# The last tile of a recommendation tower: an order of its own, four banks for its product rounds, its pair chunks one by one, and one store of all results as rows

## The chip, the core and the metric

One core of a Trainium2 chip. The core has a matrix engine (PE, called TensorE), a vector engine (DVE), an activation engine (ACT), a general engine (POOL, called GpSimd) and a queue engine that only issues transfers (SP, SyncE). They run at the same time and wait for each other on semaphores. The metric is the device time of one execution of the kernel in microseconds (us), smaller is better; a time is given as the median of several runs. Besides, one execution was recorded by the hardware profiler, and all rows below are from it.

## What is computed

For each of 2048 samples, 27 rows of 128 numbers are fetched from 27 tables by index. The rows and the products of every two of them (351 pairs), together with 16 context numbers, go through three dense layers:

```
e = stack([tbl_f[ids[:, f]] for f in range(27)], axis=1)      # 2048 x 27 x 128
inter = einsum('bfd,bgd->bfg', e, e)[:, TRIU_I, TRIU_J]        # 351 pair products
h = concatenate([e.reshape(2048, -1), inter, dense_ctx], 1)    # 3823 columns
h = maximum(h @ W_top1 + b_top1, 0)                            # 512
h = maximum(h @ W_top2 + b_top2, 0)                            # 256
y = h @ W_top3                                                 # 2048 x 1
```

## The kernel before

**Tiles and groups.** The samples are 16 tiles of 128 (numbered 0 to 15; tile 15 is `LAST`). The 27 features of a tile are 9 groups of three (`FEATS`, `GROUPS`). For each feature POOL issues one indirect gather (L240) of 128 rows of 512 bytes into a ring of six group buffers, so there are 432 gathers in 144 groups; POOL may run up to six groups ahead of PE's transposes.

**A group.** PE transposes its three features against the identity (`transpose_group`, L485) into a PSUM bank. ACT copies the bank twice: rounded to the high part (`copy_high`, L261) and whole into `emb` (`copy_whole`, L268). DVE then subtracts the high part, which gives the low part (`group_low`, L364). PE multiplies the group with its slice of the first layer's weights in three passes, high by high, high by low and low by high (`layer1_group`, L513 to L515, nine matmuls of 512 columns), and adds them up in the bank `p_hid1` of the tile.

**The pairs.** From `emb`, four rounds of small matmuls (`pair_products`, L573) make all products of a tile's samples in the two halves of `p_prod`, in turn; ACT copies one part of a round (`copy_first`, L287), DVE two parts (`copy_second`, L372). Once four rounds are copied, DVE transposes them in 32x32 blocks (`products_to_rows`, L378 and L379) and places the diagonals and the context columns as `pairs` (L382, L383). PE transposes the three chunks of `pairs` (L498, in the last tile L504), ACT and DVE split them into high and low, and PE multiplies them with the rest of the first layer's weights (`layer1_pairs`).

**The other layers.** DVE copies the finished `p_hid1` to `hid1` (`copy_hid1`, L400; in the last tile in halves, L411), PE transposes it (`transpose_hid1`, L544; last tile L551) into `p_hid1_t`, ACT adds the bias and cuts at zero (`relu1`, L304) and rounds (L308), DVE makes the low part (`hid1_to_low`, L404), PE does layer 2 (`layer2`, twelve matmuls of 256 columns, again L513 to L515), DVE layer 3 (`layer3`, L426 and L428). The result of a tile is one column of `y`, and SP stores it (`store_y`, L211): 128 partitions of 4 bytes each, 16 stores in all.

**The order.** All engines go through the same hand-written list of steps, `SEQUENCE`, for every tile: groups 0 to 6, the pairs of the tile before, groups 7 and 8. PE transposes two steps ahead of what it multiplies, in two banks in turn (`p_group`). Work of the tile before is hung on certain steps: rounds 1 to 3 of its products on groups 0 to 2, layer 2 of the tile before that on group 3, round 0 of the tile's own products and `transpose_hid1` of the tile before on group 8. The last tile has nobody behind it, so `last_tile` puts what is left after it. Each engine executes its own instructions strictly in the order written.

Of the kernel before, what the change touches and what calls it, by code (L numbers as in the profile page):

```python
# [11 lines left out]
P = 128  # L12
# [18 lines left out]
def dlrm_tower(nc, ids, tables, ctx_rows, w_dense, w_pairs, b1_t, w2, b2, w3, eye, out):  # L31
# [17 lines left out]
    FEATS = 3  # L49
# [13 lines left out]
    STEPS = len(SEQUENCE)  # L63
# [3 lines left out]
    out_t = out.rearrange("(t p) o -> t p o", p=P)  # L67

    with ExitStack() as ctx:
# [40 lines left out]
        y = sb("y", [P, TILES, 1])  # L110
# [6 lines left out]
        last_hid1_t = [p_hid1_t, p_group[1]]  # L117
# [34 lines left out]
        y_ready = sem("y_ready")  # L152

# [10 lines left out]
        LAST = TILES - 1  # L164
# [5 lines left out]
        def bank_of(g):  # L170
            return p_group[SEQUENCE.index(g) % 2][:, 0:FEATS, :]

        pairs_bank = p_group[SEQUENCE.index("pairs") % 2][:, 0:3, :]
        last_pairs_bank = [p_group[0][:, 0, :], p_prod[:, 0, 0:P], p_prod[:, 1, 0:P]]

        def steps(first_tile=0):
            return [(t, n) for t in range(first_tile, TILES) for n in SEQUENCE if t or n != "pairs"]
# [4 lines left out]
        diagonals = bass.AP(products, ROWS_Q, [[WIDE * ROWS_Q, P], [ROWS_Q + 1, NF], [ROWS_Q, DELTAS]])  # L182

        def round_products(r):

            return p_prod[:, r % 2, 0:BLOCKS * 2 * NF].rearrange("p (k u c) -> p u c k", u=2, c=NF)
# [7 lines left out]
        def _(sp):  # L194
# [30 lines left out]
            for t in range(TILES):  # L225
                store_y(t)
            sp.wait_ge(y_stored, TILES * 16)
# [18 lines left out]
        def _(act):  # L246
# [11 lines left out]
            def copy_high(t, g):  # L258
                s = t * GROUPS + g
                wait(act, group_used, s - SPLIT + 1)  # L260
                nc.scalar.activation(emb_high[:, s % SPLIT, :, :], bank_of(g),  # L261
                                     ACT.Copy).then_inc(group_high_done, 1)

            def copy_whole(t, g):
                if g == 0:
# [3 lines left out]
                                     bank_of(g), ACT.Copy).then_inc(group_copied, 1)  # L269
# [13 lines left out]
            def copy_first(t, r):  # L283
# [3 lines left out]
                nc.scalar.activation(round_columns(r), round_products(r)[:, 0], ACT.Copy).then_inc(first_copied, 1)  # L287

            def pairs_high(t):
                act.wait_ge(pairs_transposed, t + 1)  # L290
                wait(act, hid1_done, t)
                nc.scalar.activation(inter_high[:], pairs_bank, ACT.Copy).then_inc(inter_high_done, 1)
# [24 lines left out]
            order = steps()  # L317
            group_copies(0, 0)
            group_copies(0, 1)
            for k, (t, n) in enumerate(order):  # L320
                if k + 2 < len(order):
# [359 lines left out]
```

## Time and profile before

| | us |
|---|---|
| median of 3 runs | 590.93 |
| the runs | 589.64 to 592.48 |
| the profiled execution, whole | 588.81 |
| its span, first to last instruction | 586.7 |
| PE busy | 516.8 (88%) |
| POOL busy | 413.3 (70%) |
| ACT busy | 244.0 (42%) |
| DVE busy | 230.3 (39%) |
| granted TensorE clock, mean | 0.968 |

A share of busy time is a mean over stages that differ, and POOL's excludes the fixed stretch of about 0.3 us between two gathers. The time outside the span, 588.81 less 586.7, is 2.1 us.

### The profile page before, as it was taken

Reading aid. Unit: us, or ns where it says so; the run is one execution under the profiler, and the core shown is the slowest. Engines: PE = TensorE matmul, PEld = TensorE weight load, DVE = VectorE, ACT = ScalarE, POOL = GpSimd, SP = SyncE. Lnnn points to the kernel's source line nnn. Section 1 sums busy time; section 2 is a strip of 40 time slices with the busy share of each in tenths; the row PEclk is TensorE's granted clock in tenths of the full one; section 3 lists DMA queues with packets and bytes.
Section 4 is the critical chain, followed back from the end, with each engine's and each line's share of the span. In section 5 each row is a group of like instructions: output and inputs, shape, how many; then the busy total and the mean of one; then the engine's idle time right before and its main releaser. Section 6 shows DMA issues by size and latency. Waiting matters only on the chain.

```text
span 586.7 us, 10584 instructions
## 1 busy us (share of the span) xinstructions
PE 516.8 (88%) x4224; PEld 416.4 (71%) x4224; DVE 230.3 (39%) x476; ACT 244.0 (42%) x482; POOL 413.3 (70%) x436
## 2 busy tenths in 40 slices
PE   0668999799997989989899997999999997999973
PEld 0546787688786878778687785888787876878862
DVE  3662624324251343415134341534434241533442
ACT  3773544353433434343343432434443532444220
POOL 6777777777777777777777777777777777777200
PEclk9998999899998999989899997999999998999987
DMA  8873222423223242421525233241423233232000
GB/s 205 255 240 91 74 55 53 52 55 53 55 53 54 56 51 54 50 60 51 55 55 47 58 50 55 55 55 51 55 55 48 57 49 56 55 51 55 22 2 1
DMA packets 25748, 38.17 MB, mean 65 GB/s; under 512 B 14058, under 2 KB 14954, under 8 KB 25700
## 3 DMA queue, kind: packets, MB, share of 16 engines
q0 software_dynamic: 13824, 28.34, 26.6%
q1 hardware_dynamic: 11876, 9.16, 5.7%
q8 instruction: 34, 0.56, 0.4%
q14 instruction: 14, 0.11, 0.1%
HBM read 37.46 MB, written 0.01 MB: 64 GB/s over the span
## 4 chain that ended last, share of the span: by engine, by line
POOL 46%; PE 27%; issue 15%; DMA 9%; DVE 1%; ACT 0%; DVEq 0%; ACTq 0%; POOLq 0%
POOL gathered L240 46%; DMA gathered<-tbl_dram,idx 9%; PE p_hid L513 6%; PE p_hid L515 6%; PE p_hid L514 6%; PE p_prod L573 5%; PE p_group L485 3%; PE p_hid_t L544 1%; DMA idx<-ids_dram 0%; ACT hid L304 0%; ACT emb L268 0%; PE p_group L498 0%; DVE products L379 0%; DVE pairs L382 0%; PE p_hid_t L551 0%
## 5 line engine op out<-in xcount | busy, mean ns | idle before, releaser
L240 POOL DMA_INDIRECT gathered<-tbl_dram,idx x432 | 413.1, 956 | 133.7 <-issue 124.6
L364 DVE TENSOR_TENSOR emb_low<-p_group,emb_high 128x384 fp32r<-128x384 f32 x144 | 80.4, 558 | 292.4 <-ACT emb L268 291.6
L261 ACT ACTIVATE emb_high<-p_group 128x384 fp32r<-128x384 f32 x144 | 70.7, 491 | 282.6 <-PE p_group L485 282.6
L513 PE MATMUL p_hid<-w_high,emb_high 128*128 128x512 f32 x432 | 185.8, 430 | 0.0
L515 PE MATMUL p_hid<-w_high,emb_low 128*128 128x512 f32 x432 | 172.8, 400 | 0.0
L514 PE MATMUL p_hid<-w_low,emb_high 128*128 128x512 f32 x432 | 172.8, 400 | 0.0
L485 PE MATMUL p_group<-identity,gathered 128*128 128x128 f32 x432 | 78.0, 291 | 53.9 <-DMA gathered<-tbl_dram,idx 53.9
L268 ACT ACTIVATE emb<-p_group 128x384 f32<-128x384 f32 x144 | 125.1, 868 | 0.0
L485 PEld LDWEIGHTS p_group<-identity,gathered 128*128 128x128 f32 x432 | 51.8, 146 | 72.9 <-DMA gathered<-tbl_dram,idx 53.3
L515 PEld LDWEIGHTS p_hid<-w_high,emb_low 128*128 128x128 f32 x432 | 82.5, 191 | 20.0
L514 PEld LDWEIGHTS p_hid<-w_low,emb_high 128*128 128x128 f32 x432 | 83.6, 194 | 13.3
L513 PEld LDWEIGHTS p_hid<-w_high,emb_high 128*128 128x128 f32 x432 | 83.4, 193 | 13.4
L573 PEld LDWEIGHTS p_prod<-emb 128*64 128x64 f32 x2048 | 66.2, 140 | 24.8 <-issue 22.3
L573 PE MATMUL p_prod<-emb 128*64 128x54 f32 x2048 | 74.3, 227 | 2.3 <-ACT emb L268 2.3
L372 DVE COPY prod<-p_prod 32x216 f32<-32x216 f32 x128 | 48.8, 382 | 24.9 <-ACT prod L287 20.1
L287 ACT ACTIVATE prod<-p_prod 128x216 f32<-128x216 f32 x64 | 24.7, 387 | 6.6 <-PE p_prod L573 6.6
L355 DVE TENSOR_TENSOR w_low<-w_stage,w_high 128x512 fp32r<-128x512 f32 (+1 forms) x32 | 21.8, 693 | 10.0 <-ACT w_high L256 9.3
L256 ACT ACTIVATE w_high<-w_stage 128x512 fp32r<-128x512 f32 (+1 forms) x32 | 20.0, 635 | 11.2 <-DMA w_stage<-w_dense_dram 11.0
L513 PE MATMUL p_hid<-w_high,inter_high 126*128 126x512 f32 x48 | 21.8, 455 | 0.5 <-DVE inter_low L394 0.5
L514 PE MATMUL p_hid<-w_low,inter_high 126*128 126x512 f32 x48 | 20.6, 429 | 0.0
L515 PE MATMUL p_hid<-w_high,inter_low 126*128 126x512 f32 x48 | 20.3, 424 | 0.0
L513 PE MATMUL p_hid<-w_high,hid_high 128*128 128x256 f32 x64 | 18.3, 286 | 0.9 <-DVE hid_low L420 0.9
(48 smaller groups left out, 257.8 us busy)
## 6 DMA issues: line engine op xcount, KB each, us to landing
w_stage<-w_dense_dram SPq DMA_DIRECT2D x27, 256.0 KB, 3.4
gathered<-tbl_dram,idx POOLq DMA_INDIRECT x432
w_stage<-w_pairs_dram SPq DMA_DIRECT2D x3, 252.0 KB
w_stage<-w_dram SPq DMA_DIRECT2D x2, 256.0 KB, 5.0
out_dram<-y SPq DMA_DIRECT2D x16, 0.5 KB, 7.3
ctx_sb<-ctx_rows_dram SPq DMA_DIRECT2D x1, 216.0 KB, 6.7
idx<-ids_dram SPq DMA_DIRECT2D x1, 202.5 KB, 5.2
b_rows<-b_dram SPq DMA_DIRECT2D x1, 128.0 KB, 3.2
```

Source lines behind the costliest of these rows:

```text
L240: pool.indirect_dma_start(gathered[:, slot, k, :], None, tables[f], bass.IndirectOffsetOnAxis(ap=idx[:, t, f:f + 1], axis=0),).then_inc(gr ...
L261: nc.scalar.activation(emb_high[:, s % SPLIT, :, :], bank_of(g), ACT.Copy).then_inc(group_high_done, 1)
L268: nc.scalar.activation(emb[t % 2][:, :, f0:f0 + FEATS].rearrange("p b f -> p f b"), bank_of(g), ACT.Copy).then_inc(group_copied, 1)
L287: nc.scalar.activation(round_columns(r), round_products(r)[:, 0], ACT.Copy).then_inc(first_copied, 1)
L355: nc.vector.tensor_tensor(dst, src, high, ALU.subtract).then_inc(w_low_done, 1)
L364: nc.vector.tensor_tensor(emb_low[:, s % SPLIT, :, :], bank_of(g), emb_high_f32[:, s % SPLIT, :, :], ALU.subtract).then_inc(group_low_done, 1)
L372: nc.vector.tensor_copy(round_columns(r)[rows], round_products(r)[rows, 1]).then_inc(second_copied, 1)
L485: last = nc.tensor.transpose(bank_of(g)[:, k, :], gathered[:, slot, k, :], identity[:])
L513: nc.tensor.matmul(dst, high, w_high, start=start, stop=False)
L514: nc.tensor.matmul(dst, high, w_low, start=False, stop=False)
L515: return nc.tensor.matmul(dst, low, w_high, start=False, stop=stop)
L573: last = nc.tensor.matmul(p_prod[h * 2 * SLOT:(h + 1) * 2 * SLOT, r % 2, j * 2 * NF:(j + 1) * 2 * NF], x.rearrange("p b f -> p (b f)"), x[ ...
```

## The change

The steps of tiles 0 to 14 stay as they are. In the first 15 tiles only the stores are gone. What changes:

- **The last tile's order.** `LAST_SEQUENCE` puts the pairs of tile 14 after group 4 and not after group 6. Within the last tile PE transposes a group one step ahead and not two. `transpose_hid1` of tile 14 moves from behind group 7 to behind group 5, `layer2` of tile 14 from behind the last product round to ahead of the first one, and the multiplications of groups 7 and 8 move from ahead of and between the product rounds to behind all four.
- **Four banks.** The rounds 2 and 3 of the last tile's products go into the bank of tile 14's finished `p_hid1` and into `p_hid1_t`, so that no round waits for the copies of an earlier one.
- **Pair chunks one by one.** For the last tile ACT, not DVE, places the diagonals, in three pieces; the first needs only the first of DVE's two block transposes. PE transposes chunk 0 while it still has two features of group 8 to multiply.
- **One store.** `y` has 128 columns, of which 16 are used and the rest zeroed at the start. At the end PE transposes `y`, DVE copies 16 rows of 128 numbers to `y_rows`, and SP stores them with one transfer of 16 rows of 512 bytes.

```diff
-    STEPS = len(SEQUENCE)
+    LAST_SEQUENCE = [0, 1, 2, 3, 4, "pairs", 5, 6, 7, 8]
+    ORDER = [(t, n) for t in range(TILES) for n in (LAST_SEQUENCE if t == LAST else SEQUENCE) if t or n != "pairs"]
-    out_t = out.rearrange("(t p) o -> t p o", p=P)
+    out_t = out.rearrange("(t p) o -> t (p o)", p=P)
...
-        y = sb("y", [P, TILES, 1])
+        y = sb("y", [P, P])
+        y_rows = sb("y_rows", [TILES, P])
...
+        last_prod_bank = [p_prod[:, 0, :], p_prod[:, 1, :], p_hid1[(LAST - 1) % 2][:],
+                          p_hid1_t[:].rearrange("p c b -> p (c b)")]
...
-            def store_y(t):
-                sp.wait_ge(y_ready, t + 1)
-                sp.dma_start(out_t[t], y[:, t, :]).then_inc(y_stored, 16)
...
-            for t in range(TILES):
-                store_y(t)
-            sp.wait_ge(y_stored, TILES * 16)
+            sp.wait_ge(y_copied, 1)
+            sp.dma_start(out_t, y_rows[:]).then_inc(y_stored, 16)
+            sp.wait_ge(y_stored, 16)
...
+            def last_place_pairs(t):
+
+                for c in range(3):
+                    act.wait_ge(rows_done, 2 * t + min(c, 1) + 1)
+                    nc.scalar.activation(pairs[:, c * ROWS_I:(c + 1) * ROWS_I, 0:DELTAS], diagonals(c * ROWS_I, ROWS_I),
+                                         ACT.Copy).then_inc(last_placed, 1)
...
+                    if (ahead_t, ahead) == (LAST, GROUPS - 2):
+                        relu1(LAST - 1)
...
-            products_to_rows(LAST)
+            last_products_to_rows(LAST)
+            layer3(LAST - 1)
             last_pairs_low(LAST)
-            layer3(LAST - 1)
...
+            dve.wait_ge(y_transposed, 1)
+            nc.vector.tensor_copy(y_rows[:], y_bank[0:TILES, :]).then_inc(y_copied, 1)
...
+            def last_tile(t):
...
+                layer1_group(t, 3)
+                layer2(t - 2)
+                transpose_pairs(t - 1)
+                transpose_group(t, 5)
+                layer1_group(t, 4)
+                layer1_pairs(t - 1)
+                transpose_group(t, 6)
+                layer1_group(t, 5)
                 transpose_hid1(t - 1)
+                transpose_group(t, 7)
+                layer1_group(t, 6)
+                transpose_group(t, 8)
                 layer2(t - 1)
+                for r in range(ROUNDS):
+                    pair_products(t, r)
+                layer1_group(t, 7)
+                layer1_group(t, 8, [0])
+                last_transpose_pairs(t, [0])
+                layer1_group(t, 8, [1, 2])
+                last_transpose_pairs(t, [1, 2])
+                layer1_pairs(t, by_chunk=True)
                 last_transpose_hid1(t)
                 layer2(t, by_chunk=True)
+                pe.wait_ge(y_ready, TILES)
+                nc.tensor.transpose(y_bank, y[:], identity[:]).then_inc(y_transposed, 1)
```

**PE at the four product rounds of tile 15.** A row is one instruction or a run of equal ones. Before, from `transpose_hid1` of tile 14 (L544) over the transposes of group 8 (L485) and two rounds (L573) to the multiplication of group 8 (L513):

```order
2054 L544 MATMUL p_hid_t<-identity,hid 128x128 [waits hid1_relu_done,hid1_copied]
2055 L544 MATMUL p_hid_t<-identity,hid 128x128 x3
2056 L485 MATMUL p_group<-identity,gathered 128x128 [waits inter_low_done,group_gathered_5]
2057 L485 MATMUL p_group<-identity,gathered 128x128 x2
2058 L573 MATMUL p_prod<-emb 64x54 [waits second_copied,group_copied]
2059 L573 MATMUL p_prod<-emb 64x54 x15
2060 L573 MATMUL p_prod<-emb 64x54 [waits second_copied]
2061 L573 MATMUL p_prod<-emb 64x54 x15
2062 L513 MATMUL p_hid_1<-w_high,emb_high 128x512 [waits group_low_done]
```

Now, the same engine, from the last matmul of layer 2 of tile 14 over the four rounds (now L620) to the multiplication of group 7:

```order
2060 L555 MATMUL p_hid<-w_high,hid_low 128x256
2061 L620 MATMUL p_prod<-emb 64x54 [waits second_copied,group_copied]
2062 L620 MATMUL p_prod<-emb 64x54 x15
2063 L620 MATMUL p_prod<-emb 64x54 [waits second_copied]
2064 L620 MATMUL p_prod<-emb 64x54 x15
2065 L620 MATMUL p_hid_0<-emb 64x54 [waits hid1_copied]
2066 L620 MATMUL p_hid_0<-emb 64x54 x15
2067 L620 MATMUL p_hid_t<-emb 64x54 [waits hid1_relu_done]
2068 L620 MATMUL p_hid_t<-emb 64x54 x15
2069 L553 MATMUL p_hid_1<-w_high,emb_high 128x512 [waits group_low_done]
```

The rounds stand together, rounds 2 and 3 wait for semaphores of tile 14, and layer 2 of tile 14 stands ahead of them.

**DVE between the low parts of groups 6 and 8 of tile 15.** Before, L364 is `group_low`, L400 `copy_hid1` and L404 `hid1_to_low` of tile 14:

```order
364 L387 TENSOR_TENSOR inter_low<-p_group,inter_high 128x384 [waits inter_high_done]
365 L364 TENSOR_TENSOR emb_low<-p_group,emb_high 128x384 [waits group_copied,group_high_done]
366 L400 COPY hid<-p_hid_0 128x512 [waits hid1_low_done,hid1_done]
367 L404 TENSOR_TENSOR hid_low<-hid,hid_high 128x512 [waits hid1_high_done]
368 L364 TENSOR_TENSOR emb_low<-p_group,emb_high 128x384 [waits group_copied,group_high_done]
```

Now (L388, L431 and L435 are the same three steps):

```order
367 L431 COPY hid<-p_hid_0 128x512 [waits hid1_low_done,hid1_done]
368 L388 TENSOR_TENSOR emb_low<-p_group,emb_high 128x384 [waits group_copied,group_high_done] x2
369 L435 TENSOR_TENSOR hid_low<-hid,hid_high 128x512 [waits hid1_high_done]
370 L388 TENSOR_TENSOR emb_low<-p_group,emb_high 128x384 [waits group_copied,group_high_done]
371 L396 COPY prod<-p_prod 32x27x8 [waits first_copied]
```

The low part of `hid1`, on which layer 2 of tile 14 waits, now stands behind the low parts of groups 6 and 7.

**PE at the pair chunks of tile 15.** Before, from the end of layer 2 of tile 14 to the multiplication of the chunks:

```order
2086 L515 MATMUL p_hid<-w_high,hid_low 128x256
2087 L504 MATMUL p_group<-identity,pairs 126x2x2x32 [waits pairs_placed]
2088 L504 MATMUL p_prod<-identity,pairs 126x2x2x32 x2
2089 L513 MATMUL p_hid_1<-w_high,inter_high 128x512 [waits inter_low_done]
2090 L514 MATMUL p_hid_1<-w_low,inter_high 128x512
```

Now, from the last pass of the first feature of group 8:

```order
2080 L555 MATMUL p_hid_1<-w_high,emb_low 128x512
2081 L549 MATMUL p_group<-identity,pairs 126x2x2x32 [waits group_low_done,last_placed]
2082 L553 MATMUL p_hid_1<-w_high,emb_high 128x512 [waits group_low_done]
2083 L554 MATMUL p_hid_1<-w_low,emb_high 128x512
2084 L555 MATMUL p_hid_1<-w_high,emb_low 128x512
2085 L553 MATMUL p_hid_1<-w_high,emb_high 128x512
2086 L554 MATMUL p_hid_1<-w_low,emb_high 128x512
2087 L555 MATMUL p_hid_1<-w_high,emb_low 128x512
2088 L549 MATMUL p_prod<-identity,pairs 126x2x2x32 [waits last_placed] x2
2089 L553 MATMUL p_hid_1<-w_high,inter_high 128x512 [waits inter_low_done]
```

Chunk 0 is transposed six matmuls earlier than the other two.

## Rows read from the trace of the kernel before

**Rows 1.** The chain that ended last, section 4 of the page, by engine.

```profile
POOL 46%; PE 27%; issue 15%; DMA 9%; DVE 1%; ACT 0%; DVEq 0%; ACTq 0%; POOLq 0%
```

**Rows 2.** Timeline of POOL: start us, us, engine, line, operation, idle before.

```profile
79.61 0.94 POOL L240 DMA_INDIRECT gathered<-tbl_dram,idx  x1 [0.30 <-issue]
...
90.84 0.95 POOL L240 DMA_INDIRECT gathered<-tbl_dram,idx  x1 [0.30 <-issue]
...
520.07 0.95 POOL L240 DMA_INDIRECT gathered<-tbl_dram,idx  x1 [0.30 <-issue]
...
546.31 0.95 POOL L240 DMA_INDIRECT gathered<-tbl_dram,idx  x1 [0.30 <-issue]
```

**Rows 3.** Timeline of PE, the transposes of five of the 144 groups.

```profile
82.13 0.55 PE L485 MATMUL p_group<-identity,gathered 128*128 128x128 f32 x3
...
94.45 0.55 PE L485 MATMUL p_group<-identity,gathered 128*128 128x128 f32 x3 [0.91 <-DMA gathered<-tbl_dram,idx]
...
217.34 0.55 PE L485 MATMUL p_group<-identity,gathered 128*128 128x128 f32 x3 [1.47 <-DMA gathered<-tbl_dram,idx]
...
487.08 0.55 PE L485 MATMUL p_group<-identity,gathered 128*128 128x128 f32 x3 [4.18 <-DMA gathered<-tbl_dram,idx]
...
525.68 0.49 PE L485 MATMUL p_group<-identity,gathered 128*128 128x128 f32 x3
```

**Rows 4.** Waits of PE from 100 to 530 us: us in total, times, longest.

```profile
PE p_group L485 <- DMA gathered<-tbl_dram,idx: 26.9, 13, 4.2
```

**Rows 5.** A store (timeline), all stores' landing, and the load of the identity.

```profile
478.77 0.33 SPq L211 DMA_DIRECT2D out_dram<-y  x1
...
DMA to landing us min/median/max: 6.8/7.3/10.3
...
identity<-eye_dram SPq DMA_DIRECT2D x1, 64.0 KB, 1.8
```

**Rows 6.** Three stretches: us, busy by engine, then PEclk, DMA share, GB/s.

```profile
217.00:222.00 5.00, 4.66 (x23) 3.87 (x24) 0.84 (x2) 2.53 (x4) 3.78 (x4) 1.00 0.26 63
484.00:487.00 3.00, 0.00 (x0) 0.00 (x0) 0.00 (x0) 0.00 (x0) 2.39 (x3) 1.00 1.00 37
559.21:562.70 3.49, 3.49 (x64) 3.41 (x64) 1.32 (x3) 0.62 (x2) 0.00 (x0) 0.52 0.02 5
```

**Rows 7.** Timeline of PE from group 7 of tile 15 to its pair chunks.

```profile
553.89 0.40 PE L513 MATMUL p_hid<-w_high,emb_high 128*128 128x512 f32 x1
...
555.99 0.60 PE L544 MATMUL p_hid_t<-identity,hid 128*128 128x128 f32 x4
556.42 0.49 PE L485 MATMUL p_group<-identity,gathered 128*128 128x128 f32 x3
...
559.21 3.58 PE L573 MATMUL p_prod<-emb 128*64 128x54 f32 x64 [2.30 <-ACT emb L268]
...
565.00 2.08 PE L573 MATMUL p_prod<-emb 128*64 128x54 f32 x64
...
568.41 0.28 PE L515 MATMUL p_hid<-w_high,hid_low 128*128 128x256 f32 x1
570.57 0.33 PE L504 MATMUL p_group<-identity,pairs 128*126 128x128 f32 x1 [1.87 <-DVE pairs L383]
```

**Rows 8.** Timeline of ACT and DVE over the same end.

```profile
549.89 0.49 ACT L261 ACTIVATE emb_high<-p_group 128x384 fp32r<-128x384 f32 x1 [1.93 <-PE p_group L485]
...
551.24 0.56 DVE L364 TENSOR_TENSOR emb_low<-p_group,emb_high 128x384 fp32r<-128x384 f32 x1 [2.69 <-ACT emb L268]
...
556.62 1.14 ACT L304 ACTIVATE hid<-p_hid_t,b_sb 128x128 f32<-128x128 f32 x4 [5.48 <-PE p_hid_t L544]
...
558.46 0.69 DVE L404 TENSOR_TENSOR hid_low<-hid,hid_high 128x512 fp32r<-128x512 f32 x1 [3.68 <-ACT hid_high L308]
...
574.05 0.76 DVE L411 COPY hid<-p_hid 128x256 f32<-128x256 f32 x2 [1.27 <-PE p_hid L515]
...
578.94 0.08 DVE L428 DVE_READ_ACCUMULATOR hid<-hid,w_rows 128x1 f32 x1
```

More of the change, by code:

```diff
@@ L332, in _ @@
                     relu1(t - 2)
-                if n in (0, 1, 2, 3) and t >= 1:
+                if n in (0, 1, 2, 3) and 1 <= t < LAST:
                     copy_first(t - 1, n)
@@ L492, in transpose_pairs, with last_transpose_pairs @@
             def transpose_pairs(t):
-                before = SEQUENCE[SEQUENCE.index("pairs") - 2]
                 pe.wait_ge(pairs_placed, 2 * (t + 1))
-                pe.wait_ge(group_low_done, (t + 1) * GROUPS + before + 1)
+                wait_for_bank(t + 1, "pairs")
                 for c in range(3):
-                    last = nc.tensor.transpose(by_sample(pairs_bank[0:K_PAIR, c, :]), chunk_columns(c), identity[:])
+                    last = nc.tensor.transpose(by_sample(bank_of(t + 1, "pairs")[0:K_PAIR, c, :]), chunk_columns(c),
+                                               identity[:])
                 last.then_inc(pairs_transposed, 1)
-            def last_transpose_pairs(t):
-                pe.wait_ge(pairs_placed, 2 * (t + 1))
-                for c in range(3):
+            def last_transpose_pairs(t, chunks):
+                for c in chunks:
+                    pe.wait_ge(last_placed, 2 + c)
+                    if c == 0:
+                        pe.wait_ge(group_low_done, t * GROUPS + GROUPS - 1)
                     nc.tensor.transpose(by_sample(last_pairs_bank[c][0:K_PAIR, :]), chunk_columns(c),
                                         identity[:]).then_inc(pairs_transposed, 1)
-            def landings(t, g, par):
-                first = (par * GROUPS + g) // RING + 1
-                return first + (t - par) * GROUPS // RING if isinstance(t, int) else first + (t - par) // 2 * 3
             def three_passes(dst, high, low, w_high, w_low, start, stop):
@@ L515, in three_passes, with layer1_group @@
                 return nc.tensor.matmul(dst, low, w_high, start=False, stop=stop)
-            def layer1_group(t, g, par, first=False):
+            def layer1_group(t, g, feats=range(FEATS)):
                 s = t * GROUPS + g
@@ L562, in layer2, with pair_products @@
                 last.then_inc(hid2_done, 1)
-            def pair_products(t, par, r):
+            def pair_products(t, r):
                 if r == 0:
                     pe.wait_ge(group_copied, (t + 1) * GROUPS)
-                wait(pe, second_copied, (t * ROUNDS + r - 1) * HALVES)
+                if t == LAST and r == 2:
+                    pe.wait_ge(hid1_copied, LAST)
+                elif t == LAST and r == 3:
+                    pe.wait_ge(hid1_relu_done, LAST * C1)
+                else:
+                    wait(pe, second_copied, (t * ROUNDS + r - 1) * HALVES)
+                bank = last_prod_bank[r] if t == LAST else p_prod[:, r % 2, :]
                 for j in range(BLOCKS):
@@ L576, in pair_products, with tile @@
                 last.then_inc(round_done, 1)
-            def tile(t, par, depth=2):
-                other = (par + 1) % 2
-                order = [n for n in SEQUENCE if depth or n != "pairs"]
-                for at, n in enumerate(order):
-                    if at + 2 >= len(order):
-                        transpose_group(t + 1, at + 2 - len(order), other)
-                    elif order[at + 2] == "pairs":
-                        transpose_pairs(t - 1)
+            def tile(t):
+                for n in SEQUENCE:
+                    if (t, n) not in ORDER:
+                        continue
+                    ahead_t, ahead = ORDER[ORDER.index((t, n)) + 2]
+                    if ahead == "pairs":
+                        transpose_pairs(ahead_t - 1)
@@ L641, in _ @@
-            tile(LAST - 1, 0)
-            last_tile(LAST, 1)
+            pe.wait_ge(zeroed, 3)
+            transpose_group(0, 0)
+            transpose_group(0, 1)
+            for t in range(LAST):
+                tile(t)
+            last_tile(LAST)
 N_TABLES = 27
```

186 lines of the change are left out of this document (95 added, 91 removed).

## The prediction, made before the changed kernel ran

> **What bounds the kernel now.** I read the chain that ended last first. By engine POOL carries 46% and PE 27% of it [rows 1]: for most of the span the pace is that of the gathers, and only the end is PE's. The timeline of POOL shows that pace: a gather takes 0.95 us and the next starts 0.30 us later [rows 2], 1.25 us each, 3.75 us for a group, 33.75 us for a tile of nine groups. The last one is out at 546.31 + 0.95 = 547.26 [rows 2]. PE needs less: its busy time is 516.8 us in the table, 32.3 us a tile, so PE could gain at least 1.4 us a tile on POOL.
>
> Then I measured how far PE is behind: the start of a group's transposes less the end of its third gather. For group 1 of tile 2 it is 82.13 - (79.61 + 0.94) = 1.58 us, without a wait [rows 2, 3]. For group 1 of tile 15 it is 525.68 - (520.07 + 0.95) = 4.66 us [rows 2, 3], although thirteen tiles lie between. Something holds PE back. The waits name it: between 100 and 530 us PE waits 13 times for a gather, 26.9 us in all, up to 4.2 us [rows 4]. In the timeline each of the 13 ends 7.1 to 10.8 us after the start of a store of `y`; the reader can follow one pair, the store at 478.77 [rows 5] and the wait of 4.18 us that ends at 487.08 [rows 3]. In between, the stretch from 484 to 487 us shows the DMA engines fully busy (share 1.00) while they move 37 GB/s, where the calm stretch from 217 to 222 us has a share of 0.26 for 63 GB/s [rows 6]. A store takes 6.8 to 10.3 us to land [rows 5]. I read this as the gathers behind a store being held up while its 128 pieces of 4 bytes are written.
>
> The third part is the end. From 525.68 us PE has no recorded wait until the transposes of group 8 end at 556.42 + 0.49 = 556.91. Then it idles 2.30 us, and the first two product rounds take 3.58 us where the second two take 2.08 [rows 7]; the granted clock in the first stretch is 0.52 of 2.4 GHz, so the lower level of 1.2 GHz for nearly all of it [rows 6]. Behind the last round PE finishes layer 2 of tile 14 at 568.69 and idles 1.87 us for the pairs [rows 7]. The copies of the finished first layer start at 574.05, the last result is there at 579.02 [rows 8], and the span ends 7.7 us later, at 586.7: the last store, which lands in 6.8 us or more [rows 5].
>
> **Part 1, fifteen stores fewer beside the gathers.** They go from tiles 0 to 14. If they cause the stalls, PE comes up to the floor that a gather's own landing sets. What is that floor? The only wait past the start-up that no store precedes ends at 94.45, and gives 94.45 - (90.84 + 0.95) = 2.66 us [rows 2, 3]; the smallest distance without a wait is the 1.58 us above. So group 1 of tile 15 starts 4.66 - 2.66 = 2.0 to 4.66 - 1.58 = 3.1 us earlier; I take **2.5**. If the stores are not the cause, it is 0. POOL itself gains nothing, since it never waits long. PE would then wait in each tile for what it gains on POOL, about 1.4 us; after a wait of 1.47 us the clock stays at 1.00 [rows 3, 6], so I add nothing for it. Zeroing `y` at the start is one DVE instruction while PE waits for its first gather, which hides it.
>
> **Part 2, the last tile's order.** Up to the end of group 8's transposes PE does the same work as before except the multiplication of group 7, which now comes later. That is 555.99 - 553.89 = 2.10 us [rows 7], so they end at 556.91 - 2.10 = 554.8 (times here are those of the old trace; part 1 shifts them all by 2.5). This holds if the new order makes no wait on the way. The tightest place is the transposes of group 5: they need the low part of group 4, which DVE computes behind the placing of tile 14's pairs; by my estimate both are ready within 0.3 us of PE, and I put 0.1 on it (rival d has the rest). The gathers are no limit: group 8 lands by 547.26 + 2.66 = 549.9, PE asks at 554.5, or 552.0 with part 1.
>
> What is queued behind what then? `transpose_hid1` of tile 14 now ends two transposes and one multiplication ahead, at about 554.8 - 2.8 = 552.0. ACT needs 558.46 - 556.62 = 1.84 us for the four biases and the rounding, then 551.24 - 549.89 = 1.35 for group 7's copies [rows 8]; DVE does group 7's low part (0.56) and only then the low part of `hid1` (0.69) [rows 8]. Layer 2 of tile 14 can start at 552.0 + 1.84 + 1.35 + 0.56 + 0.69 = 556.4, while PE is free at 554.8: **a new wait of 1.6 us** ahead of layer 2, in place of the old one of 2.30. Behind the queue on DVE stands group 8's low part, which nobody needs before 564. Layer 2 takes 1.5 us (568.69 less the end of the rounds at 567.08, drain left out), and the four rounds twice 2.08 plus 0.1 for the waits on semaphores, since none waits for copies any more: they end at 556.4 + 1.5 + 4.2 = 562.1, where they ended at 565.00 + 2.08 = 567.08 [rows 7]. **Gain 5.0.** This contains the old half-speed rounds (3.58 - 2.08 = 1.5), which I expect to go, because the wait of 1.6 is near the 1.47 that left the clock alone and under the 2.30 that did not [rows 3, 6, 7].
>
> **Part 3, the pair chunks.** From the last round to the copies of the first layer it took 574.05 - 567.08 = 6.97 us [rows 7, 8]. Now PE has real work in that stretch: two multiplications of groups (4.2), three transposes (0.35) and the chunks' nine matmuls, which are as many as a group's (2.1), in all 6.7. Chunk 0 is asked for after 2.10 + 0.70 = 2.8 us. The old path from the last round to placed pairs took 570.57 - 567.08 = 3.5 us [rows 7]. The new one needs only the first block transpose and a third of the diagonals, and I estimate 2.7; were it 3.5, PE would idle 0.7. ACT and DVE split chunk 0 meanwhile. I take 6.9, so **0.1** gained, between 0.3 and -0.6. Layer 3 of tile 14 now stands ahead of the chunks' low parts on DVE; ACT makes chunk 0's high part in that time, so it delays nothing that PE wants before chunk 1 is in.
>
> **Part 4, one store at the end.** Added: one PE transpose with its semaphore, 0.33 to 0.5 us, and one DVE copy of 16x128, at most the 0.4 of a 128x256 one [rows 8]; 0.8 in all. The new store has 16 rows of 512 bytes. No row shows such a write. The near end is the load of the identity, also 512-byte rows, in 1.8 us; the far end is the old store's 6.8 to 7.3 [rows 5]. The size of the pieces is what differs most from the old store, so I take the load and add 0.5 for the write's direction, 2.3: 7.0 - 2.3 - 0.8 = **3.9** gained, bounds 4.4 and -0.8. The Trainium skill, "DMA: Bandwidth & Descriptors", Specifications, gives 512 bytes as the least for full rate and says that smaller pieces are read, modified and written; Anatomy of one DMA there gives a fixed part of about 2.0 us, most of it the target's receipt. By that estimate the new store lands in 2.0 us, and the sum would be 0.3 better; the trace agrees that 4-byte pieces land in more than three times that.
>
> **The sum.** 2.5 + 5.0 + 0.1 + 3.9 - 0.1 = 11.4 us. On the profiled execution's own 588.81 (span 586.7 and 2.1 around it) that gives 577.4. The median of the runs is 590.93, 2.1 above. Part of that will be stalls that fell less luckily, which the change takes away, so I carry half: **578.5**.
>
> **The rivals.** (a) The stalls stay: something else that comes once a tile, not the store, holds the gathers. For it speaks only that some stores are followed by no wait (PE was then far behind); against it the 13 of 13. It gives 578.5 + 2.5 = 581.0. (b) The row store lands as slowly as the old one, because a write's receipt costs that whatever its size: 578.5 + 4.7 = 583.2. (c) The new wait of 1.6 us lowers the clock after all: the rounds and some of layer 2 at half speed cost 1.5 to 3 us, 580 to 581.5. (d) The order does not do what it says: chunk 0 comes late (0.7) and the group 5 place waits for DVE (up to 1.5), 580.7. (e) Slower than before: the clock falls at the new wait and does not come back before the first layer ends. The work behind the wait is 1.5 + 4.2 + 6.7 = 12.4 us at full speed, and at half speed it costs 12.4 more, 578.5 + 12.4 = 590.9; with a late chunk 0 it is slower than the median. It decides once more than 11.4 us of that work run at 1.2 GHz. Against it: before, after a longer idle of 2.30 us, the rounds from 565.00 on ran at full speed again [rows 7].
>
> **How the numbers follow.** Chances: forecast 0.53, (a) 0.15, (b) 0.11, (c) 0.11, (d) 0.07, (e) 0.03. The likeliest case alone spans 575.5 to 580.5 by the bounds of parts 1, 3 and 4 and the share of the 2.1. The range reaches to (a), (b), (c) and (d): 575.0 to 583.5, with (e), combinations of two rivals and the tail beyond left out. A measurement of this kernel can tell a change of about 0.5% (3 us) from none. Every case but (e) lies 7 us or more below the median; two or more rivals together could come near it. So faster 0.94, same 0.03, slower 0.03.
>
> **What would show it.** Right if, after: PE's waits for gathers are many and short (no DMA share near 1.00 past the start), and group 1 of tile 15 starts at 522.6 to 523.7; layer 2 of tile 14 is preceded by a wait of 1 to 2 us that ends with DVE's low part; the 128 product matmuls run at a PEclk near 1.00; PE has no wait over 0.5 us between the last round and the end of the chunks; the last result is near 571.5, the end of the span 3.1 us later. Wrong if the DMA share still peaks once a tile, if the rounds show 0.5, or if the last store's landing exceeds 4 us.

## The result, and the profile after

The changed kernel takes 575.77 us in the median of four runs (574.69 to 577.27), the kernel before 591.70 beside it (589.64 to 593.10). The ratio is 0.973, with a 95% interval of 0.970 to 0.977: 2.7% less time. The profiled execution took 575.93 us with a span of 573.8, where the one before took 588.81 with 586.7. The span is 12.9 us shorter; the sum of the prediction was 11.4. One of the ten runs of e2 below took 717.05 us at a mean granted clock of 0.66 and is left out of its figures.

Where it went is read in the same order as before. First the page: the DMA row in 40 slices, and what the queue of the gathers (q0) and the queue of SP (q1) took of the 16 DMA engines.

```profile
PE 511.9 (89%) x4225; PEld 406.4 (71%) x4225; DVE 229.5 (40%) x476; ACT 245.8 (43%) x486; POOL 413.6 (72%) x436
...
DMA  8883211111111112121111121111111111111100
...
q0 software_dynamic: 13824, 28.34, 17.3%
q1 hardware_dynamic: 9604, 9.16, 5.5%
...
POOL 61%; issue 20%; PE 14%; DMA 3%; DVE 1%; ACT 0%; DVEq 0%; POOLq 0%
```

For comparison, the queue rows of before:

```profile
q0 software_dynamic: 13824, 28.34, 26.6%
```

The gathers are the same 13,824 packets and the same 28.34 MB, but they hold the DMA engines for 17.3% of the span and not for 26.6%. (In the other seven traces below that have no small store beside the gathers it is 17.2 to 19.5%.) The chain of after (the last row of the first fence) now has POOL with 61% where it was 46% [rows 1]: the kernel follows the gathers more closely, and PE's own part of the chain has halved.

The same shows in PE's waits from 100 to 530 us. They add up to as much as before, but they are 32 and not 13, and none is longer than 1.3 us where one was 4.2 [rows 4]:

```profile
PE p_group L528 <- DMA gathered<-tbl_dram,idx: 28.2, 32, 1.3
```

The long waits had a second price, which neither the prediction nor its rows name: behind six of them, of 2.3 to 4.2 us, the clock of the kernel before stood at 0.50 to 0.64 for some 4 us. This is the stretch behind the wait of 2.29 us that ends at 286.13 us:

```profile
286.10:290.00 3.90, 3.87 (x12) 3.16 (x13) 0.56 (x1) 1.24 (x2) 2.99 (x4) 0.56 0.35 84
```

Such stretches are much of why the mean granted clock was 0.968 and is now 0.993.

Group 1 of tile 15 in the timelines of POOL and PE, to be held against [rows 2, 3], and the windows for [rows 6]; the third window is that of the four product rounds:

```profile
519.77 0.94 POOL L247 DMA_INDIRECT gathered<-tbl_dram,idx  x1 [0.31 <-issue]
...
546.52 0.95 POOL L247 DMA_INDIRECT gathered<-tbl_dram,idx  x1 [0.30 <-issue]
```

```profile
522.28 0.55 PE L528 MATMUL p_group<-identity,gathered 128*128 128x128 f32 x3 [1.13 <-DMA gathered<-tbl_dram,idx]
```

```profile
217.00:222.00 5.00, 3.88 (x43) 2.78 (x43) 0.92 (x2) 1.26 (x2) 3.78 (x5) 1.00 0.19 52
484.00:487.00 3.00, 2.21 (x11) 1.89 (x12) 0.94 (x2) 1.26 (x2) 2.33 (x3) 1.00 0.19 55
554.75:558.70 3.95, 3.95 (x130) 3.89 (x129) 2.00 (x6) 1.05 (x3) 0.00 (x0) 1.00 0.02 6
```

PE is now 522.28 - 520.71 = 1.57 us behind POOL, practically the smallest distance seen before (1.58), where it was 4.66. The stretch from 484 to 487 us, in which the DMA engines had a share of 1.00 and PE did nothing, is like any other.

The end of tile 15 on PE, from the transposes of group 8 to the last result, answers to [rows 7]:

```profile
551.10 0.49 PE L528 MATMUL p_group<-identity,gathered 128*128 128x128 f32 x3
553.18 0.36 PE L553 MATMUL p_hid<-w_high,hid_high 128*128 128x256 f32 x1 [1.59 <-DVE hid_low L435]
...
554.75 2.08 PE L620 MATMUL p_prod<-emb 128*64 128x54 f32 x64
556.66 1.10 PE L620 MATMUL p_hid<-emb 128*64 128x54 f32 x32
557.60 1.10 PE L620 MATMUL p_hid_t<-emb 128*64 128x54 f32 x32
561.55 0.33 PE L549 MATMUL p_group<-identity,pairs 128*126 128x128 f32 x1
```

The new wait of 1.59 us ahead of layer 2 of tile 14 is there, and it ends with DVE's low part of `hid1`. The rounds follow each other without a gap and at a clock of 1.00. Chunk 0 of the pairs (561.55) is transposed without a wait, where PE had waited 1.87 us. On DVE and SP the last steps answer to [rows 8] and [rows 5]:

```profile
565.77 0.76 DVE L442 COPY hid<-p_hid 128x256 f32<-128x256 f32 x2 [1.56 <-PE p_hid L555]
...
571.05 0.08 DVE L459 DVE_READ_ACCUMULATOR hid<-hid,w_rows 128x1 f32 x1
571.70 0.28 DVE L508 COPY y_rows<-p_group 16x128 f32<-16x128 f32 x1 [0.57 <-PE p_group L685]
```

```profile
DMA to landing us min/median/max: 1.4/1.4/1.4
```

The last result is there at 571.13, its store starts at 572.00 and lands in 1.4 us (second fence), and the span ends at 573.8.

### The profile page after: what moved, and what is told of

Read it like the earlier page. It is cut to its first block, busy times and chain, and to the rows that moved or that the text cites. A ratio compares the mean times of both kernels' runs of the same rounds, so it can differ in the third digit from the quotient of the medians.

```text
span 573.8 us, 10576 instructions
## 1 busy us (share of the span) xinstructions
PE 511.9 (89%) x4225; PEld 406.4 (71%) x4225; DVE 229.5 (40%) x476; ACT 245.8 (43%) x486; POOL 413.6 (72%) x436
## 3 DMA queue, kind: packets, MB, share of 16 engines
q0 software_dynamic: 13824, 28.34, 17.3%
## 4 chain that ended last, share of the span: by engine, by line
POOL 61%; issue 20%; PE 14%; DMA 3%; DVE 1%; ACT 0%; DVEq 0%; POOLq 0%
POOL gathered L247 61%; PE p_hid L553 3%; DMA gathered<-tbl_dram,idx 3%; PE p_hid L554 3%; PE p_hid L555 3%; PE p_prod L620 2%; PE p_group L528 2%; DMA idx<-ids_dram 0%; PE p_hid_t L585 0%; PE p_group L540 0%; PE p_hid L620 0%; PE p_hid_t L620 0%; ACT hid L323 0%; ACT emb L275 0%; DVE hid_low L435 0%
## 5 line engine op out<-in xcount | busy, mean ns | idle before, releaser
L388 DVE TENSOR_TENSOR emb_low<-p_group,emb_high 128x384 fp32r<-128x384 f32 x144 | 80.3, 558 | 287.5 <-ACT emb L275 287.5
L528 PEld LDWEIGHTS p_group<-identity,gathered 128*128 128x128 f32 x432 | 48.7, 143 | 80.5 <-DMA gathered<-tbl_dram,idx 64.6
L620 PEld LDWEIGHTS p_prod<-emb 128*64 128x64 f32 x1984 | 62.8, 138 | 22.0 <-issue 21.8
L620 PE MATMUL p_prod<-emb 128*64 128x54 f32 x1984 | 70.7, 224 | 0.0
L396 DVE COPY prod<-p_prod 32x216 f32<-32x216 f32 x124 | 47.3, 382 | 28.7 <-ACT prod L294 25.3
L263 ACT ACTIVATE w_high<-w_stage 128x512 fp32r<-128x512 f32 (+1 forms) x32 | 20.1, 633 | 11.7 <-DMA w_stage<-w_dense_dram 11.4
L553 PE MATMUL p_hid<-w_high,inter_high 126*128 126x512 f32 x48 | 20.4, 424 | 0.0
L555 PE MATMUL p_hid<-w_high,inter_low 126*128 126x512 f32 x48 | 19.0, 395 | 0.0
L554 PE MATMUL p_hid<-w_low,inter_high 126*128 126x512 f32 x48 | 18.9, 395 | 0.0
```

The source lines that it names most:

```text
L388: nc.vector.tensor_tensor(emb_low[:, s % SPLIT, :, :], bank_of(t, g), emb_high_f32[:, s % SPLIT, :, :], ALU.subtract).then_inc(group_low_d ...
L396: nc.vector.tensor_copy(round_columns(r)[rows], round_products(t, r)[rows, 1]).then_inc(second_copied, 1)
L528: last = nc.tensor.transpose(bank_of(t, g)[:, k, :], gathered[:, slot, k, :], identity[:])
L553: nc.tensor.matmul(dst, high, w_high, start=start, stop=False)
L554: nc.tensor.matmul(dst, high, w_low, start=False, stop=False)
L555: return nc.tensor.matmul(dst, low, w_high, start=False, stop=stop)
```

## The experiments

In e1 to e4 a kernel is made of one part of the change, or the changed kernel gets stores added. Times are medians. The kernel before, run beside them, took 590.02 us with e1 to e4, 593.17 with e5 to e8 and 590.05 with e9, and gains are counted from it. The start of the gathers differs by up to 2.5 us between executions: the last gather starts at 544.35 us in one and at 546.83 in another, for the same instructions. So parts of a microsecond are compared as the distance from the start of the last gather to the last result, which is 579.02 - 546.31 = 32.7 us before and 571.13 - 546.52 = 24.6 after. Across the two orders this flatters the new one by 0.5 us: from the third gather of group 1 of tile 15 to the last gather it is 26.2 us in the kernel before and in e1, and 26.7 in the changed kernel, where two gathers take longer (last section).

**e1, the store alone** (kernel before, with the one store as rows):

```diff
-            for t in range(TILES):
-                store_y(t)
-            sp.wait_ge(y_stored, TILES * 16)
+            sp.wait_ge(y_copied, 1)
+            sp.dma_start(out_t, y_rows[:]).then_inc(y_stored, 16)
+            sp.wait_ge(y_stored, 16)
```

> The kernel before with the one store of rows alone; order, banks and pair chunks stay. Theory (the small stores hold up gathers, and land slowly at the end): group 1 of tile 15 starts with a distance of about 1.6 us to its last gather (4.66 before, 1.57 after), the end from last result to end of span takes about 2.7 us (7.7 before), and the time is 8 to 11 us under before's median of 591.7, so 581 to 584. Rival (the stalls come from something else once a tile): the distance stays at 3 to 5 us, the waits for gathers stay at 2 to 4 us each, and only 5 us are gained, 586 to 587.

It takes 579.73 us (579.42 to 580.51), ratio 0.984 (0.980 to 0.988), span 577.3. Its waits for gathers from 100 to 530 us, its PE from the transposes of group 8 on, and the stretch of the first two rounds in windows:

```profile
PE p_group L488 <- DMA gathered<-tbl_dram,idx: 27.6, 34, 1.3
```

```profile
553.67 0.49 PE L488 MATMUL p_group<-identity,gathered 128*128 128x128 f32 x3
556.46 2.08 PE L576 MATMUL p_prod<-emb 128*64 128x54 f32 x64 [2.30 <-ACT emb L267]
...
566.32 0.33 PE L507 MATMUL p_group<-identity,pairs 128*126 128x128 f32 x1 [1.87 <-DVE pairs L382]
```

```profile
556.46:560.00 3.54, 3.54 (x71) 3.21 (x72) 2.08 (x5) 0.97 (x3) 0.00 (x0) 1.00 0.03 7
```

The gain of 10.3 us is the 8 to 11 expected. With the order untouched the long waits for gathers are gone, so the stores made them. The two waits of the old order, 2.30 and 1.87 us, stay. But behind the same 2.30 us the rounds now run at a clock of 1.00 and take 2.08 us, where they ran at 0.52 and took 3.58 before [rows 6, 7]. So a wait of 2.30 us does not by itself bring the clock down. From the last gather to the last result it takes 28.2 us: of the 32.7 of before, 4.5 went without any new order: 3.1 of PE's distance from POOL and 1.5 of slow rounds are 4.6.

**e2, the order alone** (changed kernel, but with the 16 stores of columns and without the transpose of `y`):

```diff
-            sp.wait_ge(y_copied, 1)
-            sp.dma_start(out_t, y_rows[:]).then_inc(y_stored, 16)
-            sp.wait_ge(y_stored, 16)
+            for t in range(TILES):
+                sp.wait_ge(y_ready, t + 1)
+                sp.dma_start(out_c[t], y[:, t:t + 1]).then_inc(y_stored, 16)
+            sp.wait_ge(y_stored, TILES * 16)
```

> The changed kernel with the 16 small column stores of before, and without the transpose of y at the end: the new order, four banks and pair chunks alone. Theory: 4.9 us from the order remain as gain; the distance at group 1 of tile 15 goes back to 3 to 8 us, the end takes 7.7 us again, and the time is 584 to 588. Rival: the order alone keeps the gathers free; then the distance stays 1.6 us and the time is 581.

It takes 585.45 us (584.12 to 587.89), ratio 0.992 (0.989 to 0.995). The long waits for gathers are back, and the landing of 7 us and more; the first two rounds run at full speed here too; and a wait of 2.12 us for a gather, which ends at 523.58, leaves the clock at 1.00:

```profile
PE p_group L528 <- DMA gathered<-tbl_dram,idx: 27.4, 13, 5.0
```

```profile
DMA to landing us min/median/max: 6.8/7.7/11.1
```

```profile
558.47 2.08 PE L620 MATMUL p_prod<-emb 128*64 128x54 f32 x64
```

```profile
523.60:527.00 3.40, 3.40 (x18) 2.86 (x19) 0.56 (x1) 1.68 (x4) 2.68 (x3) 1.00 0.27 71
```

PE is 526.06 - 520.64 = 5.42 us behind POOL at group 1 of tile 15. The order as such gains 590.02 - 585.45 = 4.6 us, the store 10.3; together 14.9. The whole change gained 15.9 in its own comparison and 18.6 beside e5; the nearest measure, e4, which ran with these two, gained 14.6. The parts add up within what such medians can tell, although e1 and e2 each contain the 1.5 us of rounds brought back to full speed.

**e3, fifteen small stores put back** (changed kernel, and besides a column of `y` stored after each of tiles 0 to 14, which the last store overwrites):

```diff
+            for t in range(TILES - 1):
+                sp.wait_ge(y_ready, t + 1)
+                sp.dma_start(out_c[t], y[:, t:t + 1]).then_inc(y_stored, 16)
```

> The changed kernel with 15 column stores of 128 pieces of 4 bytes put back beside it (tiles 0 to 14, as each result is ready); the store of rows at the end stays, and overwrites them. Theory: DMA share near 1.00 for some us once a tile, waits of PE for gathers of 1 to 4 us each 7 to 11 us behind a store, distance at group 1 of tile 15 from 3 to 8 us, and the time 3 to 6 us over the changed kernel's 575.8, 579 to 582. Rival: no stalls, 576.

It takes 583.00 us (581.24 to 584.00), 1 us beyond what was expected, and 7.5 more than the kernel with other extra stores, below. The waits, and two stretches in windows:

```profile
PE p_group L533 <- DMA gathered<-tbl_dram,idx: 31.5, 13, 6.1
```

```profile
484.00:487.00 3.00, 3.00 (x18) 2.45 (x16) 0.56 (x1) 1.52 (x3) 2.14 (x3) 1.00 0.89 34
523.00:526.00 3.00, 1.93 (x6) 1.70 (x7) 0.00 (x0) 0.99 (x2) 2.39 (x3) 0.66 0.47 75
```

The DMA share is back at 0.89 for 34 GB/s. PE is 528.06 - 522.31 = 5.75 us behind at group 1 of tile 15, and in the second stretch, after a wait of 2.20 us, its clock is 0.66 for a while. The last store alone still lands in 1.4 us.

**e4, fifteen stores of whole rows instead** (changed kernel, and after each of tiles 0 to 14 a store of 16 rows of 512 bytes of zeros, overwritten at the end):

```diff
+            for t in range(TILES - 1):
...
+                sp.wait_ge(y_ready, t + 1)
+                sp.dma_start(out_t, filler[:]).then_inc(y_stored, 16)
```

> The changed kernel with 15 stores of 16 rows of 512 bytes (zeros, overwritten at the end) at the same places. Theory (it is the 4-byte pieces, not a write to memory beside the gathers): no stall, distance 1.6 us at group 1 of tile 15, each store lands in 1.4 to 3 us, time 576 within 1 us. Rival (any write holds up the gathers): waits as with the small ones, 579 to 582.

It takes 575.46 us (574.83 to 575.61), as if they weren't there:

```profile
PE p_group L537 <- DMA gathered<-tbl_dram,idx: 27.5, 31, 1.2
```

```profile
484.00:487.00 3.00, 2.96 (x15) 2.11 (x14) 1.32 (x3) 1.39 (x3) 2.39 (x3) 1.00 0.25 66
```

So neither a store beside the gathers nor its bytes (8 KB here, 0.5 KB there) holds them up; PE is 522.48 - 520.93 = 1.55 us behind at group 1 of tile 15. The store of 128 pieces of 4 bytes does. Whether it is the size of the pieces, their number, or that all of them fall into one stretch of 512 bytes was not tried. Against the number alone speaks only that each gather, too, is 128 pieces, of 512 bytes, and follows the next without such stalls.

**e9, the small stores held back until the gathers are over** (changed kernel with the 16 stores of columns, all behind one wait):

```diff
+            sp.wait_ge(group_transposed, TILES * GROUPS)
+            for t in range(TILES):
+                sp.wait_ge(y_ready, t + 1)
+                sp.dma_start(out_c[t], y[:, t:t + 1]).then_inc(y_stored, 16)
```

> The changed kernel, but with the old form of store (one column of y, 128 pieces of 4 bytes, 16 of them, no transpose of y), and all of them held back on the queue engine until the last group has been transposed, at about 551 us. If the 4-byte stores are what holds the gathers up, then nothing is held up here although the number and form of stores is that of the kernel before: PE is 1.5 to 1.6 us behind POOL at group 1 of tile 15, and no wait for a gather is over 1.3 us between 100 and 530 us. The end then tells the two prices of such a store apart. If its 7 us of landing are a delay and not work, fifteen of them issued in a row from 551 us are done before the last result is there (571 us), the last one lands 7 to 8 us behind its result, and the span ends near 579. If its 7 us are work of the DMA engines (they were at a share of 1.00 for 3 us and more after each store of the kernel before), fifteen in a row queue up for 15 x 3 us or more, and the span ends at 596 us or later. The rival (it was not the stores beside the gathers): PE is 4 us or more behind POOL at group 1 of tile 15, with waits over 3 us.

The span is 580.1 us, where 579 was expected, and the time 582.79 (two runs). Waits for gathers; then all stores, from the first at 550.69 to the end of the last one's issue; then the stretch in which fifteen of them were written, in windows; and the queues:

```profile
PE p_group L529 <- DMA gathered<-tbl_dram,idx: 28.4, 31, 1.2
```

```profile
550.69 22.20 SPq L236 DMA_DIRECT2D out_dram<-y  x16
```

```profile
551.00:566.00 15.00, 11.51 (x165) 9.81 (x166) 7.84 (x19) 4.05 (x12) 0.00 (x0) 1.00 0.11 3
```

```profile
q0 software_dynamic: 13824, 28.34, 17.2%
q1 hardware_dynamic: 11876, 9.16, 5.6%
```

This tells three things. The number and form of the stores is that of before, and no gather is held up: PE is 521.39 - 519.86 = 1.53 us behind at group 1 of tile 15. The fifteen stores in a row are no 3 us of work each: they occupy 0.11 of the engines for 15 us, about 0.11 us of all sixteen per store, and their 2,272 further packets lift SP's queue from 5.5 to 5.6%. What was occupied before was the gathers' own queue, 26.6% and not 17%: their packets stood longer. And the last store ends the span 580.1 - 572.53 = 7.6 us behind its result, with nothing beside it, so the 7 us of landing are not contention with gathers.

One thing of this run was not expected: PE stops for 1.76 and 0.48 us in the fourth round, and the trace names no releaser. It makes the last result 2.3 us later against the last gather than in the changed kernel. In the same stretch the issue of one store on SP takes 3.92 us, where 0.33 to 0.43 is usual, and ends 0.2 us from where PE goes on, while the DMA engines do nearly nothing:

```profile
554.90 3.92 SPq L236 DMA_DIRECT2D out_dram<-y  x1
```

```profile
558.60 0.26 PE L621 MATMUL p_hid_t<-emb 128*64 128x54 f32 x1 [1.76 <-issue]
```

```profile
556.00:558.50 2.50, 0.84 (x30) 0.71 (x26) 0.96 (x3) 0.30 (x1) 0.00 (x0) 1.00 0.03 3
```

It looks as if the same thing held both up, which would be a second price of such stores; no run shows what it was.

**e5, the changed kernel again**, as the base of e6, e7 and e8:

> The changed kernel once more, as the measure for the runs beside it: 575.8 within 1 us by both theories.

574.60 us (573.27 to 575.80), ratio 0.969 (0.966 to 0.972), 0.2 below the expected band. The last gather starts at 544.35 and the last result is there at 568.58: 24.2 us.

**e6, the low part of `hid1` one group earlier**, one number on DVE, aimed at the new wait:

```diff
-                    if (ahead_t, ahead) == (LAST, GROUPS - 1):
+                    if (ahead_t, ahead) == (LAST, GROUPS - 2):
```

> The changed kernel with one step of DVE moved: the low part of the first layer of tile 14 ahead of the low part of group 7 of tile 15. In the changed kernel PE waits 1.59 us for it ahead of layer 2 of tile 14. Theory (it is only queued behind group 7's low part, which waits for ACT): the wait goes, and with it 1.3 to 1.6 us, 574.3. Rival (PE then waits for group 8's copies ahead of the product rounds instead): under 0.3 us gained, 575.6.

573.36 us (571.95 to 574.23), ratio 0.966 (0.963 to 0.969), the best of all. The low part on DVE, and PE from the transposes of group 8 to the rounds:

```profile
551.00 0.69 DVE L435 TENSOR_TENSOR hid_low<-hid,hid_high 128x512 fp32r<-128x512 f32 x1 [2.45 <-ACT hid_high L327]
```

```profile
551.39 0.49 PE L528 MATMUL p_group<-identity,gathered 128*128 128x128 f32 x3
553.42 2.08 PE L620 MATMUL p_prod<-emb 128*64 128x54 f32 x64
```

The low part is made as soon as ACT has the high part. From the transposes of group 8 to the rounds it takes 2.03 us and not 3.65: the wait of 1.59 is gone, whole. From the last gather to the last result it takes 569.41 - 546.83 = 22.6 us, 1.65 less than in the kernel above. The medians differ by 1.24 us, which is at the edge of what they can tell; the timeline shows it beyond that.

**e7, two banks for the rounds** (changed kernel, but rounds 2 and 3 wait for the copies of rounds 0 and 1):

```diff
-                bank = last_prod_bank[r] if t == LAST else p_prod[:, r % 2, :]
+                bank = p_prod[:, r % 2, :]
```

> The changed kernel with the last tile's four product rounds in the two halves of one bank, in turn, so that rounds 2 and 3 wait for the copies of rounds 0 and 1. Theory: a round is made in 0.95 us and copied in 0.35 (ACT) and 0.80 us (DVE) behind it, so rounds 2 and 3 each wait about 0.9 us, 1.5 to 2 us in all, 577.5. Rival (the copies keep up, and the banks are worth nothing in this order): within 0.3 us of the changed kernel.

575.73 us (574.18 to 577.50), 1.1 over e5 where 1.5 to 2 or under 0.3 were expected. PE's rounds:

```profile
555.08 2.08 PE L615 MATMUL p_prod<-emb 128*64 128x54 f32 x64
557.50 2.08 PE L615 MATMUL p_prod<-emb 128*64 128x54 f32 x64 [0.34 <-DVE prod L396]
```

The four rounds take 4.50 us from first to last and not 3.95. By the timeline the two further banks are worth 0.55 us, less than was expected: PE waits once, for 0.34 us, and not twice for 0.9. The 1.1 between the medians is at the edge of what they can tell.

**e8, the pairs placed whole** (changed kernel, but DVE places the diagonals in one copy behind both block transposes):

```diff
-            last_place_pairs(LAST)
...
+                dve.wait_ge(rows_done, 2 * (t + 1))
+                dve.wait_ge(pairs_transposed, t)
+                nc.vector.tensor_copy(pairs[:, :, 0:DELTAS], diagonals(0, NF)).then_inc(last_placed, 3)
```

> The changed kernel with the last tile's diagonals placed in one copy by DVE behind both block transposes, PE's order unchanged. Theory: chunk 0 is placed at 2.8 us plus 0.5 behind the last round, PE asks for it at 2.8, so PE idles 0.4 to 0.7 us and the time is 576.3. Rival: the place decides nothing, since PE has other work: within 0.2 us.

575.79 us (574.83 to 576.45), 1.2 over e5. PE at chunk 0:

```profile
560.96 0.33 PE L551 MATMUL p_group<-identity,pairs 128*126 128x128 f32 x1 [0.44 <-DVE pairs L416]
```

A wait of 0.44 us comes back. From the start of the rounds to the copies of the first layer it takes 565.21 - 553.58 = 11.63 us, against 563.61 - 552.58 = 11.03: placing in pieces is worth 0.6 us. The profiled executions differ by 574.83 - 573.27 = 1.56 us, of which 0.98 is the later start of the gathers here.

## Why the prediction was right, and where its terms were off

It said 578.5 us with 575.0 to 583.5 around it; 575.77 was measured. Of the 2.7 us of error 1.5 lie in the sum (12.9 for 11.4) and 1.2 in how the sum was carried to the median.

- **What bounded the kernel.** Right. The stores of 4-byte pieces held the gathers up: e1 and e9 take them away from the gathers, e3 puts them back, and e4 puts others in their place. One word was wrong: "while its 128 pieces of 4 bytes are written" reads as if the writing filled the engines. Written alone, fifteen in a row left them nearly idle (share 0.11); it is the gathers' packets that take longer beside them. By what mechanism, no run here tells.
- **Part 1, 2.5 predicted.** Measured 4.66 - 1.57 = 3.1. The mis-sized step is the floor: of its two bounds, 2.66 and 1.58 us, the lower one was the truth, and the mean was taken. The 2.66 came from a single wait early in the run; without the small stores PE is 1.5 to 1.6 us behind at this place. Group 1 started at 522.28, just ahead of the 522.6 to 523.7 that was to show it. POOL was 0.3 us earlier besides, which is within what its start varies.
- **Part 2, 5.0 predicted.** From group 1 of tile 15 to the end of the rounds it took 567.08 - 525.68 = 41.40 us, and now 558.70 - 522.28 = 36.42: 4.98. The new wait was put at 1.6 us and measured 1.59, behind the very instruction that was named. The 0.1 put on group 5 did not show. Beside the old stores, in e2, the same stretch takes 562.41 - 526.06 = 36.35, a gain of 5.05. But the reason given for 1.5 of it, the slow rounds, does not hold. They were to be fast because the new wait is shorter than the old one. In e1, with the store alone, the old wait of 2.30 us is still there and they are fast; in e2, with the order alone, they are fast too; slow they are in the one trace of the kernel before. So the 1.5 can't be put down to the order, and that the term met its 5.0 with it is in part luck. Counted from e1, whose rounds are fast, the order gives 39.96 - 36.39 = 3.6 us over this stretch in e5; the distance from the last gather to the last result falls by 4.0 there (28.2 to 24.2), of which 0.5 is the later last gather. A wait of this length went either way: after 2.29 and 2.30 us in the kernel before, and after 2.20 in e3, the clock fell (0.56, 0.52 and, in a window that begins inside the wait, 0.66); after 2.30 in e1 and 2.12 in e2 it stayed at 1.00. The Trainium skill, "TensorE: Matmul & The Clock Gate", Part 1, says that the moments at which the chip judges PE's activity are not tied to the kernel's start. By that rule the same wait costs or spares the clock as it falls. The five cases agree with it; they do not show that this is the reason.
- **Part 3, 0.1 predicted.** Measured 565.77 - 558.70 = 7.07 for 6.97: -0.1. Chunk 0 was in time. The price of the undone half in e8, 0.6, shows that without the pieces it would have been -0.7.
- **Part 4, 3.9 predicted.** From the last result to the end of the span it took 7.7 us, now 573.8 - 571.13 = 2.7: 5.0. The hop was 0.87 as put (0.8). The mis-sized term is the landing, 1.4 us for 2.3: neither bound held it, since even the load of the identity took 1.8. The 0.5 added for the write's direction had no row behind it. The old store's end was 0.2 longer than the 7.0 put for it: its last landing took 7.2. The estimate of 2.0 us from the Trainium skill, which the prediction gave beside, was nearer, and still 0.6 too long; the section that it comes from is on transfers that GpSimd issues, and this store is SP's.
- **Not in the sum.** From the copies of the first layer to the last result it took 4.97 us before and 5.36 after. The last matmuls of layer 2 ran at a clock of 0.75 on average:

```profile
567.89:570.20 2.31, 2.31 (x12) 1.97 (x12) 1.15 (x5) 0.00 (x0) 0.00 (x0) 0.75 0.00 0
```

In e4 to e8 the same stretch took 4.97. So these 0.4 us are of this execution and not of the change. The terms come to 3.1 + 0.3 + 5.0 - 0.1 - 0.4 + 5.0 = 12.9.
- **The median.** Half of the 2.1 us between profiled execution and median was carried. The stalls that fall differently from run to run were named as the reason, and they are gone: the kernel before spreads over 588.11 to 596.45 us in all its runs, the changed one over 573.27 to 577.27. That the spread came from the stalls is likely, but no run shows it. After the change the median lies 0.2 under the profiled execution; nothing was to be carried.

Of the rivals, (a) is out, since no wait for a gather is over 1.3 us; (b) by the landing of 1.4; (c) and (e) by a clock of 1.00 in the rounds; (d) because neither chunk 0 nor group 5 found a wait.

## What to carry to other kernels

A store of a column, one small number per partition, is cheap for the engine that issues it (0.33 us) and was dear for others here: of the 13 issued before while gathers ran, 12 were followed by waits of PE of 0.9 to 4.2 us, and as the last step it put the end 7.7 us behind the last result, where one store of rows needs 2.7. Keep such results on the chip, transpose them once into rows of 512 bytes, and write them with one store. Look at the clock behind a wait before you price the wait, and in more than one trace: 2.3 us of idling went either way here. When an order is rewritten, go through each queue for a result that is ready but stands behind work nobody wants yet; the wait that this prediction had found in the new order was taken away by moving one step on one engine.

## What the runs showed of the hardware beyond that

- Sixteen rows of 512 bytes land in 1.4 us; 128 pieces of 4 bytes need 6.8 to 11.1 us, and 7.6 us from result to end with nothing else on the queues. The Trainium skill, "DMA: Bandwidth & Descriptors", Anatomy of one DMA, gives a fixed part of about 2.0 us for a transfer that GpSimd issues; here a whole store issued by SP takes less, and for it the measurement decides.
- Share of the DMA engines is not work. The same 13,824 packets of gathers filled 26.6 to 27.6% of the span in the three traces with small stores beside them and 17.2 to 19.5% in the eight without, at the same pace of POOL.
- In eight of the nine traces with the new order (not in that of e3) two gathers of tile 15 take 1.16 to 1.39 us where nearly all others past tile 1 take 0.95; in e1 none of tile 15 does, and in the kernel before one, its first (1.21 at 513.56 us, beside DVE's placing of the pairs). In the trace of after they lie beside DVE's subtraction and its placing of the pairs; in e2, where PE runs 4 us later, it is the gathers one group further on:

```profile
536.01 1.22 POOL L247 DMA_INDIRECT gathered<-tbl_dram,idx  x1 [0.30 <-issue]
...
540.04 1.19 POOL L247 DMA_INDIRECT gathered<-tbl_dram,idx  x1 [0.30 <-issue]
```

The cause was not tried. It costs nothing here, since PE asked for group 8 later than it had landed.
